# Attention stage: key tiles taken from both ends in turn, weighted sums one step at a time and four steps late

## The reference, cut to what matters

```python
b, l, d = x.shape                      # 4, 1024, 1024; 32 heads of 32
scores = jnp.einsum('bhqd,bhkd->bhqk', q, k) / math.sqrt(hd)
causal = jnp.tril(jnp.ones((l, l), bool))
scores = jnp.where(causal, scores, -jnp.inf)
att = jax.nn.softmax(scores, axis=-1)
out = jnp.einsum('bhqk,bhkd->bhqd', att, v)
```

## Time and profile before

| | us |
|---|---|
| median of 3 runs | 3147.96 (3146.01 to 3149.09) |
| the profiled execution | 3142.79 |
| its span on the core | 3140.9 |
| `attend`, first to last copy of sums, about | 1271 to 2502 |
| from the first add of group 0 to that of group 31 | 1144.6 |
| PE busy in that stretch | 1110.34 |
| ACT busy | 642.99 |
| DVE busy | 758.29 |
| POOL busy | 822.24 |

### The profile page before, as it was taken

How to read it: one execution, slowest core, us unless ns; L and a number is a source line. 1 busy time by engine, 2 the same in 40 slices (tenths; PEclk the granted TensorE clock), 3 DMA queues, 4 the chain that set the end, 5 groups by cost and what they waited for, 6 DMA issues and landing times. The chain is left out here.

```text
span 3140.9 us, 46110 instructions
## 1 busy us (share of the span) xinstructions
PE 2902.5 (92%) x16692; PEld 2043.8 (65%) x16692; DVE 1466.6 (47%) x3029; ACT 1045.4 (33%) x1442; POOL 1374.5 (44%) x701
## 2 busy tenths in 40 slices
PE   3999899989998999699999999999999869999997
PEld 2888788868887888455555555555555456767774
DVE  4121221131213111466666666666666256666664
ACT  1222312121122121155555555555555421112111
POOL 2221322242224121377766776777767613233332
PEclk7999999999999999699999999999999989999997
DMA  6444342333323543735545455555544164434431
GB/s 229 174 167 154 127 161 107 133 134 134 134 107 130 192 167 149 159 85 120 121 110 112 109 112 114 120 121 120 116 112 109 51 177 130 125 107 126 135 114 54
DMA packets 149741, 404.89 MB, mean 129 GB/s; under 512 B 17356, under 2 KB 52612, under 8 KB 148568
## 3 DMA queue, kind: packets, MB, share of 16 engines
q1 hardware_dynamic: 119272, 292.83, 27.5%
q10 hardware_dynamic: 30320, 110.15, 16.7%
HBM read 271.20 MB, written 131.20 MB: 128 GB/s over the span
## 5 line engine op out<-in xcount | busy, mean ns | idle before, releaser
L896 ACT ACTIVATE prob<-ps_s 128x1024 f32<-128x1024 f32 (+3 forms) x768 | 596.3, 812 | 447.3 <-PE ps_s L1017 361.8
L609 PE MATMUL ps_u<-h_hi,w_hi 128*128 128x512 f32 x1536 | 604.7, 394 | 0.0
L609 PE MATMUL ps_u<-h_hi,w_lo 128*128 128x512 f32 x1536 | 600.0, 391 | 0.0
L609 PE MATMUL ps_u<-h_lo,w_hi 128*128 128x512 f32 x1536 | 599.9, 391 | 0.0
L424 POOL TENSOR_TENSOR w_lo<-w_raw,w_hi 128x1024 fp32r<-128x1024 f32 x96 | 231.0, 2407 | 842.3 <-ACT w_hi L471 842.3
L852 POOL TENSOR_TENSOR added<-added,prob 128x2048 f32<-128x2048 f32 (+1 forms) x128 | 550.5, 4300 | 15.4 <-ACT prob L896 15.1
L987 PE MATMUL ps_r<-k_st,q_st 96*128 96x512 f32 (+2 forms) x1536 | 504.7, 387 | 37.0 <-DMA v_sb<-v_tok 27.5
L1017 PE MATMUL ps_s<-q_st,k_st 97*128 97x512 f32 (+2 forms) x1536 | 458.1, 380 | 24.0 <-ACT prob L896 15.4
L939 DVE TENSOR_REDUCE part_high<-ps_r 128x1 f32<-128x512 f32 x512 | 337.7, 687 | 194.3 <-PE ps_r L987 186.2
L546 DVE SCALAR_TENSOR_TENSOR qk_lo<-ps_u,bias_col,qk_hi 128x512 fp32r<-128x512 f32 x128 | 96.1, 751 | 671.9 <-ACT qk_hi L447 671.9
L987 PEld LDWEIGHTS ps_r<-k_st,q_st 96*128 96x128 f32 x1536 | 275.9, 194 | 191.7 <-issue 83.6
(11 more groups left out here) (159 smaller groups left out, 2980.0 us busy)
## 6 DMA issues: line engine op xcount, KB each, us to landing
q_st<-qk_split ACTq DMA_DIRECT2D x90, 512.0 KB, 7.7
k_st<-qk_split ACTq DMA_DIRECT2D x90, 512.0 KB, 13.7
w_raw<-w_cols SPq DMA_DIRECT2D x72, 512.0 KB, 3.5
qk_split<-qk_hi SPq DMA_DIRECT2D x64, 512.0 KB, 2.7
qk_split<-qk_lo SPq DMA_DIRECT2D x64, 512.0 KB, 3.4
xn<-in_L_attn_x SPq DMA_DIRECT2D x8, 2048.0 KB, 13.0
v_tok<-v_out SPq DMA_DIRECT2D x32, 512.0 KB, 2.7
wm<-in_L_wmod SPq DMA_DIRECT2D x8, 2048.0 KB, 8.7
```

What stands on the lines that cost most here:

```text
L609: last = nc.tensor.matmul(ps_u[u % 2][:], w[:, m, k], h[:, k, tok], start=k == 0 and j == 0, stop=k == KT - 1 and j == 2)
L896: nc.scalar.activation(prob[:, buffer_of(t, k), 2 * pair:2 * pair + 2, off:], ps_s[pair][:, :, off:], ACT.Exp, scale=SCALE).then_inc(exp_d ...
```

## The change

- The steps of each half are reordered: in place of j = 0, 1, ..., 7 it is j = 0, 7, 1, 6, 2, 5, 3, 4, and for the low half 0, 3, 1, 2. In the high half the diagonal tiles are thus steps 1, 3, 5 and 7 of a group.
- `weigh(t, k)` does one step, and is called after every step, for the step four before (HOPS = 4).
- SHARE: an even step gets 2, 1 and 1 entries of pass 1, an odd one 1, 1 and 1, so that PE has 42 as before.
- `sum_high` stands behind step 1 and `sum_low` behind step 3 of the next group, as before in time, but `sum_high` now has two terms (the adds of POOL, and step 7 with 512 columns), not three (512, 256, 128).
- POOL adds steps 2, 1, 3, 4, 5 and 6, six adds of 2048, 512, 1024, 2048, 1536 and 2048 elements, in place of five (four of 2048 and one of 1536).
- ACT's program keeps its places: the copies stand after steps 0, 1 and 3, and `load` after step 4.

```diff
-    steps = [(ch, j) for ch in reversed(range(QC)) for j in range((ch + 1) * CT)]
+    for ch in HALVES:
+        tiles = (ch + 1) * CT
+        for j in range(tiles // 2):
+            steps += [(ch, j), (ch, tiles - 1 - j)]
-    ADDS = LONG - 3
-    HOPS = 2
+    HOPS = 4
+    MASKED_STEPS = [k for k, (ch, j) in enumerate(steps) if j >= ch * CT]
+    ADDED_STEPS = (2, 1, 3, 4, 5, 6)
-    SHARE = (2, 2, 1, 1, 1)
+    SHARE = ((2, 1, 1), (1, 1, 1))
...
             for t in range(NG):
+                mask(t, 1)
+                add(t, 2)
                 add(t, 1)
-                add(t, 2)
-                mask(t, 4)
+                mask(t, 3)
                 add(t, 3)
+                add(t, 4)
                 mask(t, 5)
-                mask(t, 6)
-                add(t, 4)
+                add(t, 5)
                 mask(t, 7)
-                mask(t, 8)
-                add(t, 5)
...
+                add(t, 6)
+                for k in range(LONG, NSTEP):
+                    mask(t, k)
...
-                    act.wait_ge(weighed, before // 2 + 1)
+                    act.wait_ge(weighed, before + 1)
...
-            def weigh(t, p):
+            def weigh(t, k):
+                ch, j = steps[k]
+                off, end = offset(k), k in (LONG - 1, NSTEP - 1)
+                if k == 0 and t > 0:
                     pe.wait_ge(o_copied, 2 * t)
-                if 2 * p == LONG:
+                if k == LONG:
                     pe.wait_ge(o_copied, 2 * t + 1)
+                if k in MASKED_STEPS:
+                    pe.wait_ge(masked, masked_upto(t, k))
                 else:
+                    pe.wait_ge(exp_done, 2 * (NSTEP * t + k + 1))
...
-                for k in range(ADDS + 1, LONG):
+                k = LONG - 1
...
+                for k in range(NSTEP):
+                    turns = slots[k * TURNS:(k + 1) * TURNS]
+                    for pair in range(2):
+                        pass_1(turns[pair])
+                        if pair == 0 and k in (0, LONG):
+                            pe.wait_ge(shift_loaded[steps[k][0]], 16 * HG * (t + 1))
+                        scores(t, k, pair)
+                    pass_1(turns[2])
+                    if k >= HOPS:
+                        weigh(t, k - HOPS)
                     elif t > 0:
-                        weigh(t - 1, PAIRS - HOPS + p)
-                        (sum_high if p == 0 else sum_low)(t - 1)
+                        weigh(t - 1, NSTEP - HOPS + k)
+                        if k == 1:
+                            sum_high(t - 1)
+                        if k == HOPS - 1:
+                            sum_low(t - 1)
```

More of the change, by code:

```diff
@@ L656, in attend @@
     CT = BANK // P
-    steps = [(ch, j) for ch in reversed(range(QC)) for j in range((ch + 1) * CT)]
+    HALVES = tuple(reversed(range(QC)))
+    steps = []
+    for ch in HALVES:
+        tiles = (ch + 1) * CT
+        for j in range(tiles // 2):
+            steps += [(ch, j), (ch, tiles - 1 - j)]
     NSTEP = len(steps)
@@ L678, in attend @@
     LAG = 3
-    SHARE = (2, 2, 1, 1, 1)
+    SHARE = ((2, 1, 1), (1, 1, 1))
+    TURNS = len(SHARE[0])
     def strewn(t):
@@ L691, in per_slot @@
         todo, out = strewn(t), []
-        for n in range(PAIRS * len(SHARE)):
-            few = SHARE[n % len(SHARE)]
+        for n in range(NSTEP * TURNS):
+            few = SHARE[n // TURNS % 2][n % TURNS]
             out.append(todo[:few])
@@ L1019, in scores @@
                 last.then_inc(score_done, 1)
-            def weigh(t, p):
-                if 2 * p == 0 and t > 0:
+            def weigh(t, k):
+                ch, j = steps[k]
+                off, end = offset(k), k in (LONG - 1, NSTEP - 1)
+                if k == 0 and t > 0:
                     pe.wait_ge(o_copied, 2 * t)
-                if 2 * p == LONG:
+                if k == LONG:
                     pe.wait_ge(o_copied, 2 * t + 1)
-                if 2 * p < FIRST:
-                    pe.wait_ge(exp_done, 2 * (NSTEP * t + 2 * p + 2))
-                else:
[L1030 to L1036, removed]
+                if k in MASKED_STEPS:
+                    pe.wait_ge(masked, masked_upto(t, k))
+                else:
+                    pe.wait_ge(exp_done, 2 * (NSTEP * t + k + 1))
+                for h in range(HG):
+                    part = slice(h * HD, (h + 1) * HD)
+                    last = nc.tensor.matmul(ps_o[part, off:], v_sb[t % SLOTS][:, j, part], prob[:, buffer_of(t, k), h, off:], start=k in (0, LONG), stop=end)
                 last.then_inc(weighed, 1)
                 if end:
-                    pe.wait_ge(weighed, PAIRS * t + p + 1)
+                    pe.wait_ge(weighed, NSTEP * t + k + 1)
                     pe.sem_inc(o_done, 1)
@@ L1058, in sum_high @@
                     nc.tensor.matmul(bank_of(use)[h * HD:(h + 1) * HD, :], ones[:], added[t % 2][:, h], start=True, stop=False)
-                for k in range(ADDS + 1, LONG):
-                    off = offset(k)
-                    for h in range(HG):
-                        last = nc.tensor.matmul(bank_of(use)[h * HD:(h + 1) * HD, off:], ones[:], prob[:, buffer_of(t, k), h, off:], start=False, stop=k == LONG - 1)
+                k = LONG - 1
+                off = offset(k)
+                for h in range(HG):
+                    last = nc.tensor.matmul(bank_of(use)[h * HD:(h + 1) * HD, off:], ones[:], prob[:, buffer_of(t, k), h, off:], start=False, stop=True)
                 last.then_inc(sum_done, 1)
@@ L1068, in _ @@
                 slots = per_slot(t)
[L1069 to L1078, removed]
-                    elif t > 0:
-                        weigh(t - 1, PAIRS - HOPS + p)
-                        (sum_high if p == 0 else sum_low)(t - 1)
-            for p in range(PAIRS - HOPS, PAIRS):
-                weigh(NG - 1, p)
-                (sum_low if p == PAIRS - 1 else sum_high)(NG - 1)
+                for k in range(NSTEP):
[8 more added lines that the diff above has]
+                        weigh(t, k - HOPS)
+                    elif t > 0:
+                        weigh(t - 1, NSTEP - HOPS + k)
[3 more added lines that the diff above has]
+                            sum_low(t - 1)
+            for k in range(NSTEP - HOPS, NSTEP):
+                weigh(NG - 1, k)
+                if k == LONG + 1:
+                    sum_high(NG - 1)
+            sum_low(NG - 1)
 def finish(nc, s):
```

33 lines of the change are left out of this document (15 added, 18 removed).

## The result

The changed kernel takes 3210.84 us, median of 4 runs (3202.31 to 3216.37); the kernel before took 3148.15 in the runs beside it. Ratio 1.0198, 95% interval 1.0174 to 1.0222: slower by 63 us. The profiled executions have spans of 3200.4 and 3140.9 us, 59.5 apart, and it is these 59.5 that can be followed through the trace. The profiled execution of the changed kernel is the fastest of its four, so what the medians are apart beyond 59.5 has no rows here.

The account below looks back on a forecast made before the run. PE was taken to bound the attention stage. A period longer by 1.53 us gave +44.4 in groups 1 to 29, group 30 +0.2, group 0 nothing, the last group -4.5: +40 on 3148, so 3188 us, range 3163 to 3212.

Parts of the forecast that it names:

- the clock's fall: Rival: the 1.70 us wait per group lowers PE's granted clock, 52 us in all, 3240 us; chance 0.05.
- POOL's 3218: Rival: POOL late for the masks, 1 us a group, 3218 us; chance 0.04.
- Waits for ACT in wide steps, gone: PE's score weight loads no longer wait for ACT's wide exponents: -3.3 us a group.
- the two reasons: Why PE's general wait for ACT would end: a weigh and its block in every step, and narrow steps alternating with wide.
- Twelve blocks, 0.34 each: On PE, twelve 128*32 blocks a group in place of six, each 0.34 us beside its work: +2.04 us.
- The wait for the copy, +1.70: At a group's start, step 8's weigh on PE waits for ACT's copy out of ps_o: +1.70 us.
- The load's DMA starts, +1.30: Step 6's scores wait for ACT, which issues seven DMA starts behind step 4: +1.30 us, groups 1 to 29.
- The period: Time of one group in the attention stage: 38.45 us after the change, +1.53.
- the other waits: PE's remaining waits, such as DVE freeing the ps_r banks: 0.4 us a group, 0.3 before.
- POOL: nothing: POOL's adds take 20.7 us a group, 21.7 before, with as many masks; no cost expected.
- some 8 us in both: Last group, what follows the weigh behind step 11: some 8 us before and after the change.
- the 27.4 forecast: Last group, first score to the weigh behind step 11 or a little beyond: 27.4 us after, 31.88 before, so -4.5.

Follow-up runs that it names:

- pairs in the new order: Changed kernel with weigh for two steps in one block behind odd steps, six blocks a group: 3161.74 us, 1.005 of the kernel before.
- split pairs: Kernel weighing two steps behind odd steps in the new order, with a pass-1 entry put between the two weighs, twelve blocks a group: 3215.95 us.
- both edits in the old order: Changed kernel with the old key-tile order and its three-term sums, copy ahead of step 0's exponents, load issued by SP: 3119.77 us.

## Why the prediction was right, and where it was not

3210.84 lies in the range (3163 to 3212), at its upper end, 23 us above the forecast of 3188. The causes that carried the forecast, the blocks and the two waits, were right, and each was shown by an experiment. That the time is inside the range is in part luck: the range left the clock's fall out, the fall came in twelve groups, and an error of 9 us the other way in the period made room for some of it. Two of the four executions, 3212.84 and 3216.37, lie outside. (The range leaves out POOL's 3218 as well, so 0.23 and not 0.19 in all.)

- **Waits for ACT in wide steps, gone.** Right in size (42.2 us left, forecast about 40), but only one of the two reasons holds: the pairs in the new order keep the waits (155 us), and single steps in the old order have none (0.3 us). It is the `weigh` in every step that ends them.
- **Twelve blocks, 0.34 each.** Right: 0.35 in the timeline, 0.34 to 0.37 by the split pairs.
- **The wait for the copy, +1.70.** Right: 1.73 from start to start, and 1.73 when it is taken away.
- **The load's DMA starts, +1.30.** Too high, but inside its bounds: 1.03 by the rows, 1.15 by removal. The forecast kept the distance from step 4's exponents to step 5's; ACT issues the first start sooner, and the distance is 0.24 shorter.
- **The period.** At full clock 38.14, forecast 38.45. By removal the load's wait is 0.15 under the forecast, and the other waits are 0.22 in place of 0.4; the copy's is 0.03 over. That makes the -0.31 but for rounding. So the 30 periods gave 35.4 us, not 44.6.
- **POOL: nothing.** Right within the stage, wrong once, at its end. The forecast called the part behind step 11 "some 8 us in both". In the changed kernel the last group's masks stand behind an add of 4.5 us, and PE waits for them (no run moved them ahead of it):

```profile
2544.35 4.50 POOL L861 TENSOR_TENSOR added<-added,prob 128x2048 f32<-128x2048 f32 x1
2548.82 2.39 POOL L844 TENSOR_SCALAR_AFFINE_SELECT prob<-prob 128x512 f32<-128x512 f32 x4
```

```profile
2544.43 1.06 PE L1043 MATMUL ps_o<-prob,v_sb 128*32 128x512 f32 x8
...
2549.59 2.36 PE L1043 MATMUL ps_o<-prob,v_sb 128*32 128x512 f32 x16 [4.09 <-POOL prob L844]
```

  The last group up to the `weigh` behind step 11 takes 28.42 us (2516.01 to 2544.43; 31.88 before), near the 27.4 forecast. The 4.09 of PE's wait gives it all back.
- **The clock.** This was a rival with a chance of 0.05 and 52 us, in every group; it came in 12 groups and took some 24 us in the stage (20.7 in the table), which is the largest error of the sum. The windows view around one fall:

```profile
1811.70:1815.10 3.40, 1.74 (x12) 0.63 (x12) 1.49 (x6) 1.84 (x3) 0.00 (x0) 0.99 0.20 75
1815.10:1818.50 3.40, 3.40 (x22) 1.80 (x25) 2.08 (x3) 0.77 (x2) 0.64 (x1) 0.50 0.01 2
1818.50:1821.90 3.40, 3.40 (x28) 1.83 (x24) 1.36 (x4) 1.82 (x3) 0.00 (x0) 1.00 0.00 1
```

  In the first row PE stood 1.66 us for the copy, at 1811.93 to 1813.59, and was busy the other 1.74 at full clock; in the second it ran at 0.50, the 1.2 GHz level, with no wait; in the third at 2.4 GHz again. In those 3.40 us it does half the work: 1.7 us lost, in line with groups of 39.6 to 39.9 against 38.14. My argument against, "only one such gap in 38 us", was wrong: a single gap did it. Not always the copy's: eight of the 13 falls come right behind its 1.66, and five at the wait for the load's DMA starts, in groups in which it was 1.1 to 2.1 us (its median is 0.82). The count follows the waits: 13 with both, 5 without the copy's, 10 without the load's, 0 without either. Pairs in the new order wait longer for ACT in all (155 us), but PE by at most 0.9 at once (and once for DVE by 1.3), and have none; both edits in the old order have one fall, behind a wait of 1.20 for the shift. Why the fall comes in some groups and not in others with the same gap isn't shown by any run. It doesn't look random: with the load on SP the first six falls come every third group, 112.6 us apart.
- The 3.5 us behind the last copy stand in a stage that the change doesn't touch. There the clock's mean is lower in some windows of the changed kernel, and no experiment was made on it.

## What to carry to other kernels

When work is spread over more, smaller blocks, look for the wait that the big block covered, and ask of each engine in the handshake whether it does its release last in a step: the copy behind two exponents cost 1.7 us a group, and moving one line ahead of them took 72 us off the median; with the DMA starts moved to an idle queue too, the changed kernel became 54 us faster than the one before. The same two edits did nothing before the change, so such edits are tried after a restructuring, and not only before it. And look at the last round by itself: what a steady group hides need not be hidden there.

## What the runs showed of the hardware

- A single PE idle time of 1.66 us in 38 us of nearly full work can bring the granted clock from 2.4 to 1.2 GHz, and so did single waits of 1.1 to 2.1 us; a fall cost about 1.7 us more. Taking the copy's wait away saved 51.9 us in the periods by itself and 9.0 by the falls that went with it.
- ACT issues the first of its DMA starts while an earlier exponent still runs (1751.52 inside 1750.77 to 1751.79), so seven starts that take 3.4 us (1751.52 to 1754.90) leave it idle for 2.32.
- The price of going into and out of the 128\*32 shape was the same for blocks of either length: 0.35 us behind 2 passes, 0.34 behind 4.
